# Three float16 products in the output projection of a gated attention block, and a later wait for its transposed attention

## The reference

```
x   : [8, 256, 128]      context : [8, 512, 128]      16 heads of 64
xn  = layernorm(layernorm(x)) ; q = xn @ w_q ; k, v = split(context @ w_kv)
attn = softmax((q * 64**-0.5) @ k.T)  per head
out  = (attn @ v).reshape(8, 256, 1024)                 # the attention
x   = x + tanh(g_xattn) * tanh(gate) * (out @ w_out + b_out)   # the output projection
tokens = layernorm(x) ; expert = argmax(tokens @ gate_w), at most 160 tokens for each of 8
x   = x + tanh(g_ffn) * prob * (relu(tokens @ w1[expert]) @ w2[expert])
```

## Time and profile before

| | |
|---|---|
| runs | 473.90, 474.88, 475.59 us, median 474.88 |
| profiled execution | 473.7 us from the first to the last instruction; what lies around the span is not recorded, so that the median is 1.2 us above it |
| TensorE matmul (PE) | busy 439.7 us, 93% of the span |
| ScalarE (ACT) | 386.4 us, 82% |
| VectorE (DVE) | 360.3 us, 76% |
| GpSimd (POOL) | 356.6 us, 75% |
| granted TensorE clock | 0.996 on average, full in all stretches of the attention |
| the chain that ended last | PE 40%, DVE 20%, ACT 16%, DMA 10%, issue 8%, POOL 4% |
| share of the 16 DMA engines' time with packets of the hardware queue | 93.4% |

### The profile page before, as it was taken

One profiled execution on the slowest core, in us unless ns is written; L12 is line 12 of the kernel. 1 busy time (PEld: TensorE's weight loads), 2 busy tenths in 40 slices (PEclk: granted clock), 3 DMA queues, 4 the chain that ended last, 5 costly groups with the idle time before them and its releaser, 6 DMA issues.

```text
span 473.7 us, 13155 instructions
## 1 busy us (share of the span) xinstructions
PE 439.7 (93%) x5096; PEld 334.0 (71%) x5096; DVE 360.3 (76%) x789; ACT 386.4 (82%) x630; POOL 356.6 (75%) x270
## 2 busy tenths in 40 slices
PE   7889799998999989999999999999999999988993
PEld 6656667776767767776777667776777677758892
DVE  4787687778877887779787796878877887785622
ACT  5889788899888988899888898899799998892330
POOL 3687686888788887888878877898878877871325
PEclk9999999999999999999999999999999999999998
DMA  5499999999999999999999999999989998996021
GB/s 167 150 177 192 206 187 175 170 181 204 188 176 188 210 194 180 192 192 192 198 189 197 189 196 191 185 200 209 190 157 185 193 180 147 159 182 137 14 67 46
DMA packets 283037, 82.10 MB, mean 173 GB/s; under 512 B 264387, under 2 KB 280435, under 8 KB 282976
## 3 DMA queue, kind: packets, MB, share of 16 engines
q1 hardware_dynamic: 281600, 77.96, 93.4%
q0 software_dynamic: 1376, 3.30, 2.2%
HBM read 10.83 MB, written 5.14 MB: 34 GB/s over the span
## 4 chain that ended last, share of the span: by engine, by line
PE 40%; DVE 20%; ACT 16%; DMA 10%; issue 8%; POOL 4%; POOLq 0%; SPq 0%; ACTq 0%; DVEq 0%
DVE MXL L903 9%; DMA PT<-PARTS 9%; ACT P L752 7%; DVE HL L890 4%; ACT HL L714 4%; PE psAB L1234 3%; PE psX L1319 3%; PE psAB L1241 3%; PE psO L1267 3%; ACT PARTS L762 3%; POOL PARTS L650 3%; PE psX L1355 3%; DVE VL L896 3%; PE psO L1269 3%; PE psO L1268 3%
## 5 line engine op out<-in xcount | busy, mean ns | idle before, releaser
L650 POOL TENSOR_TENSOR PARTS<-P,PARTS 128x1024 f16<-128x1024 f32 x125 | 267.4, 2145 | 63.5 <-ACT PARTS L762 61.8
L762 ACT ACTIVATE PARTS<-P 128x1024 f16<-128x1024 f32 x126 | 136.1, 1080 | 0.7
L752 ACT ACTIVATE P<-psAB,NB 128x512 f32<-128x512 f32 x128 | 81.6, 695 | 41.8 <-DVE NB L906 41.4
L903 DVE TENSOR_REDUCE MXL<-psAB 128x2 f32<-128x1024 f32 x64 | 78.4, 1224 | 41.4 <-PE psAB L1241 23.9
L1267 PE MATMUL psO<-VH,PT 128*128 128x65 f16 x1008 | 98.6, 194 | 8.3 <-DMA PT<-PARTS 7.7
L1267 PEld LDWEIGHTS psO<-VH,PT 128*128 128x128 f16 x1008 | 92.0, 98 | 12.0 <-DMA PT<-PARTS 8.9
L1268 PE MATMUL psO<-VL,PT 128*128 128x64 f16 x1008 | 98.5, 192 | 0.0
L1269 PE MATMUL psO<-VH,PT 128*128 128x65 f16 x1008 | 98.4, 193 | 0.0
L1268 PEld LDWEIGHTS psO<-VL,PT 128*128 128x128 f16 x1008 | 91.3, 98 | 0.5
L1269 PEld LDWEIGHTS psO<-VH,PT 128*128 128x128 f16 x1008 | 91.5, 97 | 0.0
L752 ACT ACTIVATE P<-psCD,NB 128x512 f32<-128x512 f32 x128 | 81.7, 703 | 0.1
(11 more groups left out here) (214 smaller groups left out, 871.7 us busy)
## 6 DMA issues: line engine op xcount, KB each, us to landing
ctx_raw<-in_ctx_dram SPq DMA_DIRECT2D x8, 256.0 KB, 3.7
w1s<-in_L_ffn_w_dram SPq DMA_DIRECT2D x8, 256.0 KB, 3.6
w2s<-in_L_ffn_w_dram SPq DMA_DIRECT2D x8, 256.0 KB, 4.0
PT<-PARTS SPq DMA_TRANSPOSE x126, 5.0
experts_table<-zeros POOLq DMA_DIRECT2D x2, 645.0 KB, 4.0
X<-in_x_dram SPq DMA_DIRECT2D x8, 128.0 KB, 4.2
wraw<-in_L_xattn_w_kv_dram SPq DMA_DIRECT2D x4, 256.0 KB, 5.3
out_dram<-row SPq DMA_DIRECT2D x8, 128.0 KB, 2.5
```

The lines of the kernel that those rows point to most:

```text
L650: pool.tensor_tensor(PARTS[:, par, qt, 1], P32[:, par, qt], PARTS[:, par, qt, 0], ALU.subtract).then_inc(plo_done, 1)
L752: last = act.activation(P32[:, par, qt, SK * h:SK * h + SK], score_bank(qt)[:, SK * h:SK * h + SK], ACT.Exp, bias=NB[:, par, qt, h:h + 1])
L762: act.activation(PARTS[:, hp % 2, qt, 0], P32[:, hp % 2, qt], ACT.Copy).then_inc(phi_done[qt], 1)
L903: dve.tensor_reduce(MXL[:, par, qt, :, 0], score_bank(qt)[:].rearrange("p (h n) -> p h n", h=2), AX.X, ALU.max, negate=True).then_inc(max_ ...
```

## The change

- Weights: `w_out` (float32, tile `wo`) is split once into two float16 tiles: `wo_hi` = 16 * wo rounded, made by ScalarE in slot 5 of batch 0, and `wo_lo` = 16 * wo - wo_hi, made by VectorE in slot 6 of batch 0 (128 x 1024 elements each).
- Attention: the ones column by which the sums of the softmax are taken becomes 1/16, so that the normalised attention comes 16 times as large. `ot_copy` writes its transpose in float16 (`OTH`), and a new VectorE instruction in each slot, `ot_low`, subtracts that from the PSUM bank and writes the rest in float16 (`OTL`). It stands after `normalise_heads` and ahead of `token_moments` and `x_moments`, and waits for `ot_done` of this same slot's copy.
- Products: each product of a 128 x 128 tile becomes three float16 matmuls (high x high, high x low, low x high). All wait for the low part (`ot_lo_done`), save the first two of the last two pairs.
- Scale: the projection is multiplied by `gproj` = gscale / 256, one small instruction more in slot 2 of batch 0.
- Order on TensorE: `k_project` no longer waits for the attention copy; `q_project` waits instead, and for the low part.

```diff
@@ pool
-            pool.memset(VH[:, :, :, DH:DH + 2], 1.0).then_inc(row_consts, 1)
+            pool.memset(VH[:, :, :, DH:DH + 2], 1.0 / O_LIFT).then_inc(row_consts, 1)
@@ scalar
-                act.activation(OT[:, QT * pair:QT * (pair + pairs), :], bank.rearrange("p (t c) -> p t c", c=P),
+                act.activation(OTH[:, QT * pair:QT * (pair + pairs), :], bank.rearrange("p (t c) -> p t c", c=P),
                                ACT.Copy).then_inc(ot_done, pairs)
...
+                    if hp == WO_HI_STEP and is_first(b):
+                        act.wait_ge(wo_in, 16)
+                        act.activation(wo_hi[:], wo[:], ACT.Copy, scale=WO_LIFT).then_inc(wo_hi_done, 1)
@@ vector
+            def ot_low(n, bank=psOT, pairs=1):
+
+                pair = n % PAIRS
+                dve.wait_ge(ot_done, n + pairs)
+                hi = OTH[:, QT * pair:QT * (pair + pairs), :]
+                dve.tensor_tensor(OTL[:, QT * pair:QT * (pair + pairs), :], bank.rearrange("p (t c) -> p t c", c=P), hi,
+                                  ALU.subtract).then_inc(ot_lo_done, pairs)
...
                     if VALUES_BEHIND <= j < LAST:
                         normalise_heads(*back(b, hp, VALUES_BEHIND))
+                    if ot_pair(j) >= 0:
+                        ot_low(ot_pair(j))
+                    if is_first(b) and hp == WO_LO_STEP:
+                        dve.wait_ge(wo_hi_done, 1)
+                        dve.scalar_tensor_tensor(out=wo_lo[:], in0=wo[:], scalar=WO_LIFT, in1=wo_hi[:], op0=ALU.mult,
+                                                 op1=ALU.subtract).then_inc(wo_lo_done, 1)
                     if hp == PROJECT_STEP and not is_first(b):
                         token_moments(b - 1)
...
             normalise_heads(B - 1, PAIRS - 1)
+            ot_low(LAST - 2)
             normalise_heads(B - 1, PAIRS - 2)
             add_part(B - 1, B, psEF)
+            ot_low(LAST - 1, psEF[:, 512:1024], 2)
@@ tensor, k_project and q_project
-                if ot_pair(j - AHEAD - 1) >= 0:
-                    pe.wait_ge(ot_done, ot_pair(j - AHEAD - 1) + 1)
                 pe.wait_ge(ctxt_lo_done, b + 1)
...
             def q_project(b, hp):
+                j = b * PAIRS + hp
                 q_cols = slice(P * hp, P * hp + P)
+                if ot_pair(j - AHEAD - 1) >= 0:
+
+                    pe.wait_ge(ot_lo_done, ot_pair(j - AHEAD - 1) + 1)
@@ tensor, project_part (project alike)
+            PRODUCTS = ((OTH, wo_hi), (OTH, wo_lo), (OTL, wo_hi))
+
+            def project_pairs(dst, qt, pairs):
+
+                for pair in pairs:
+                    for n, (o, w) in enumerate(PRODUCTS):
+                        last = pe.matmul(dst, o[:, pair * QT + qt, :], w[:, pair, :], start=(pair == pairs[0] and n == 0),
+                                         stop=(pair == pairs[-1] and n == len(PRODUCTS) - 1))
+                return last
...
-                pe.wait_ge(ot_done, b * PAIRS + pairs[-1] + 1)
-                pe.wait_ge(wo_in, 16)
+                pe.wait_ge(ot_lo_done, b * PAIRS + pairs[-1] + 1)
+                pe.wait_ge(wo_lo_done, 1)
                 for qt in range(QT):
-                    for pair in pairs:
-                        last = pe.matmul(bank[:, D * qt:D * qt + D], OT[:, pair * QT + qt, :], wo[:, pair, :],
-                                         start=(pair == pairs[0]), stop=(pair == pairs[-1]))
+                    last = project_pairs(bank[:, D * qt:D * qt + D], qt, pairs)
@@ tensor, project_last
+                for n, (o, w) in enumerate(PRODUCTS):
+                    if n == 0:
+                        pe.wait_ge(ot_done, b * PAIRS + PAIRS)
+                    elif o is OTL:
+                        pe.wait_ge(ot_lo_done, b * PAIRS + PAIRS)
+                    for qt in range(QT):
+                        for pair in pairs:
+                            last = pe.matmul([psX, psEF][qt][:, 0:D], o[:, pair * QT + qt, :], w[:, pair, :],
+                                             start=(pair == pairs[0] and n == 0),
+                                             stop=(pair == pairs[-1] and n == len(PRODUCTS) - 1))
```

More of the change, by code:

```diff
@@ L58, in gated_block @@
     LIFT = 7.0
+    O_LIFT, WO_LIFT = 16.0, 16.0
     AHEAD = 2
@@ L85, in gated_block @@
         gscale = sb("gscale", [P, 1], F32)
+        gproj = sb("gproj", [P, 1], F32)
         w_hi = sb("w_hi", [P, 3 * INNER], F32R)
@@ L88, in gated_block @@
         wo = sb("wo", [P, PAIRS, D], F32)
+        wo_hi = sb("wo_hi", [P, PAIRS, D], F16)
+        wo_lo = sb("wo_lo", [P, PAIRS, D], F16)
         bo = sb("bo", [P, D], F32)
@@ L116, in gated_block @@
         O = sb("O", [P, QT, INNER], F32)
-        OT = sb("OT", [P, QT * PAIRS, P], F32)
+        OTH = sb("OTH", [P, QT * PAIRS, P], F16)
+        OTL = sb("OTL", [P, QT * PAIRS, P], F16)
         stats = sb("stats", [P, TT, 6], F32)
@@ L261, in gated_block @@
         ot_done = sem("ot_done")
+        ot_lo_done = sem("ot_lo_done")
+        wo_hi_done = sem("wo_hi_done")
+        wo_lo_done = sem("wo_lo_done")
         proj_psum = sem("proj_psum")
@@ L403, in gated_block @@
         BO_STEP, BIAS_STEP = 2, 7
+        WO_HI_STEP, WO_LO_STEP = 5, 6
         ROUTE = 14
@@ L943, in add_part @@
                 dve.wait_ge(part_psum, part + 1)
+                dve.wait_ge(gscale_done, 2)
                 dve.wait_ge(part_done, part)
@@ L947, in add_part @@
                 dve.scalar_tensor_tensor(out=xs, in0=bank[:, 0:QT * D].rearrange("p (q d) -> p q d", q=QT),
-                                         scalar=gscale[:, 0:1], in1=xs, op0=ALU.mult, op1=ALU.add).then_inc(part_done, 1)
+                                         scalar=gproj[:, 0:1], in1=xs, op0=ALU.mult, op1=ALU.add).then_inc(part_done, 1)
             def token_moments(b):
@@ L1092, in batch @@
                         dve.wait_ge(gscale_done, 1)
+                        dve.tensor_scalar(gproj[:], gscale[:], 1.0 / (O_LIFT * WO_LIFT), None, ALU.mult).then_inc(gscale_done, 1)
                         dve.wait_ge(bo_in, 16)
@@ L1350, in project @@
                 wait_x((x1_done, b + 1))
-                pe.wait_ge(ot_done, b * PAIRS + PAIRS)
+                pe.wait_ge(ot_lo_done, b * PAIRS + PAIRS)
                 for qt in range(QT):
-                    dst = psX[:, D * qt:D * qt + D]
-                    for pair in range(PAIRS // 2, PAIRS):
-                        last = pe.matmul(dst, OT[:, pair * QT + qt, :], wo[:, pair, :], start=(pair == PAIRS // 2),
-                                         stop=(pair == PAIRS - 1))
+                    last = project_pairs(psX[:, D * qt:D * qt + D], qt, range(PAIRS // 2, PAIRS))
                 last.then_inc(proj_psum, 1)
@@ L1402, in batch @@
                             pe.wait_ge(kq_done, LAST + 1)
-                            pe.wait_ge(ot_done, ot_pair(j))
+                            pe.wait_ge(ot_lo_done, ot_pair(j))
                         o_transposes(ot_pair(j))
@@ L1437, in batch @@
                     values(b, PAIRS - 1)
-                    pe.wait_ge(ot_done, LAST - 2)
+                    pe.wait_ge(ot_lo_done, LAST - 2)
                     o_transposes(LAST - 2)
@@ L1441, in batch @@
                     project_part(b, range(PAIRS // 2, PAIRS - 2), psEF)
-                    pe.wait_ge(ot_done, LAST - 1)
+                    pe.wait_ge(ot_lo_done, LAST - 1)
                     o_transposes(LAST - 1, psEF[:, 512:1024], 2)
```

4 lines of the change are left out of this document (2 added, 2 removed).

## The result

The changed kernel takes 479.42 us (median of seven, 478.22 to 480.31) against 474.88 for the kernel before (473.32 to 477.87). The ratio is 1.0098, 95% interval 1.007 to 1.0127: it is slower by 3.3 to 6.0 us. The forecast was 479.4. The profiled execution of after took 478.22 us, its span is 476.4, and it is the fastest of the seven; before's profiled span is 473.7 us. So the two traces differ by only 2.7 us, and the medians by 4.5. The account of the prediction comes back to this.

The account below looks back on a forecast made before the run. Bound: the loop of scores, row maximum, low part, small task and values across TensorE and VectorE. Terms 5.7 - 0.8 + 1.1 + 0.8 - 1.8 - 0.5 = +4.5 us on 473.7, span 478.2, median 479.4; range 470.0 to 484.5.

Parts of the forecast that it names:

- The mechanism: VectorE, in order: the low part waits for ScalarE's same-slot copy and delays the next row maximum; 0.36 us after each copy.
- its sign: In the profile after, VectorE's wait for ScalarE's OTH copy should be some 10 to 20 us in all.
- Rival B: The low part's wait hides, all 15 projection halves gain 0.5 us: 468.2 us; chance 0.23 with its half-way case.
- The step for slot 0: Slot 0: copy ends 5.95 us after the row maximum's start, plus 0.36 gives 6.31 against 5.98, a loss of 0.33.
- 0.2 a batch: VectorE, running later, waits less for the high part of the values; 0.2 us taken off the batch's sum.
- Rival D: Projection's float16 matmuls slower than taken, deciding from 0.079 us each; 483.6 us with no gain in a half; chance 0.10.
- 5.7 - 0.8 - 1.8: Batches 1 to 6: +5.7 us at 0.95 each, -0.8 without x moments in batch 6, -1.8 hidden in transpose waits.
- absorption in waits for transposes: Where TensorE's wait for DMA transposes sets a group of slots, the new wait hides: 0.5 in three or four batches, -1.8 us.
- the end +0.1: Last batch and end: shorter products, a low part of 512 columns, slots without value work; -0.5 us, 1.5 of doubt either way.
- the prediction's own last step: From span to median: the runs' median is 1.2 us above the profiled span, so 478.2 becomes 479.4 us.
- The weight split: Batch 0: VectorE's 1024-column instruction costs 0.8 us, part of the copy's wait using up idle time; ScalarE's costs nothing.
- Rival C: Landing of transposes sets the pace once TensorE is faster and hides the new wait: no change, 474.9 us; chance 0.14.

Follow-up runs that it names:

- run without the products: Changed kernel with the float32 products of the kernel before and no weight split, low part still made and waited for; 482.86 us, ratio 1.0172 to the kernel before.
- products alone: Changed kernel without any low-part instruction on VectorE, the third product taking the high part of the attention again; 472.4 us, ratio 0.9988 to the kernel before.
- run with the constant tile: The products-only version plus a VectorE instruction of the low part's size reading constant SBUF tiles, without the copy's wait; 501.09 us, ratio 1.0576 to the kernel before.

## Why the prediction was right, point by point

**The mechanism** was the forecast one: VectorE's in-order wait for this slot's copy. The low part starts 0.03 us behind the copy, shown above for slots 4 and 7, and the M that ends slots 2 to 5, 7 and 0 comes straight behind it or behind the moments. VectorE's wait for the copy is 27.9 us in all, more than the 10 to 20 that the prediction named as its sign. Rival B, the wait hides, falls by the run without the products: 1.0172 in place of 1 or a little over.

**The slots.** Forecast and measured (the batch above, or where it is not typical the other batches): slot 1 7.05 and 6.90; slot 2 6.71 and 6.71; slot 3 7.05 and 7.08; slot 4 6.62 and 6.62; slot 5 5.80 and 5.73; slot 6 6.03 and 6.02 (6.23 here); slot 7 6.95 and 6.89; slot 0 6.31 and 6.05. The step for slot 0 failed: it took the copy to end 5.95 after M as in the earlier trace rows, but 0.28 of that came from a short slot 7. ScalarE had the high part of the values late, VectorE waited for it, and in slot 0 the attention copy in turn waits for VectorE, which has to read the keys and queries out of the same bank (L900, done at 229.38, the copy at 229.46). With slot 7 long the copy ends 5.67 after M (229.84 less 224.17; low part at 229.88). The same step had been made for slot 5 and not for slot 0. Slot 1 is 0.15 shorter than forecast, as the projection starts 2.06 after M (180.07 less 178.01), not 2.18, and is 0.05 shorter itself. The start is earlier because VectorE, running later, finds the high part of the values there: its wait for that fell from 8.2 us in 16 waits to 3.1 in 3, by 5.1, where the forecast took off 0.2 a batch. With the products alone, where M of slot 1 isn't late, the start was still 2.18 after it and the slot 7.03.

**The products.** Timeline of TensorE in slot 1 of that batch, first and last of 24 matmuls, and the first of the values product:

```profile
180.07 0.23 PE L1351 MATMUL psX<-wo_hi,OTH 128*128 128x128 f16 x1 [0.28 <-DVE VL L910]
...
181.36 0.22 PE L1351 MATMUL psX<-wo_hi,OTL 128*128 128x128 f16 x1
181.42 0.19 PE L1301 MATMUL psO<-VH,PT 128*128 128x65 f16 x1
```

A half takes 1.35 us, forecast 1.40, by 0.056 per matmul (1.29 / 23), forecast 0.058. Scaling a float16 pace by columns held. Rival D would have needed 0.079. The figure of the Trainium skill that stood in the prediction (TensorE: Matmul & The Clock Gate, section Back-to-back issue gap: about 81 ns for 128 columns) doesn't hold here; the trace decides for 0.056.

**The terms of the sum** are less good than the total. From M of slot 1 to M of the next slot 1, after less before, the batches 0 to 6 gave +2.1, -0.8, -0.8, +0.9, +0.6, +0.9 and -0.1 us; the last batch and the tail together +0.1. For batches 1 to 6 that is +0.7, where the forecast had 5.7 - 0.8 - 1.8 = +3.1. The term that was mis-sized is the absorption in waits for transposes. Slot 7 of batches 1 and 2 was already 7.48 and 7.38 us long in before, by such a wait, and so got shorter (6.89) where +1.28 was forecast for a typical one. The traced batch, with slot 7 at 5.67, was the wrong one to multiply by six. Batch 0 gave +2.1, forecast +1.9, and the end +0.1, forecast -0.5. With the first slots 0.2 shorter, the sum over the trace is thus +2.7 and not +4.5.

That the median came out as forecast is luck, and the prediction's own last step shows where it lies. It put the median 1.2 us above the span of one execution, because before's profiled span of 473.7 was set beside the median of other executions. Wherever a run on record has both numbers of one execution, its time is 1.8 to 2.2 us above its span. By that, before's profiled execution took about 475.6 us, 0.7 above the median, and after's is 1.2 below its own. The seven spans of after have a median of 477.4. So the forecast span of 478.2 was 0.8 us too long and the step of 1.2 was 0.8 too short, and the two errors cancel. The direction and the mechanism are shown; the sum isn't.

**The weight split** in batch 0 cost about twice the 0.8 us of the forecast. Within batch 0, which has no projection, the run without the products is the changed kernel less the split. Its slot 6 takes 5.79 us, after's 7.47, and slots 5, 7 and 0 agree to 0.02. VectorE at the end of that slot, after first and then the run without the products:

```profile
59.77 0.42 DVE L943 TENSOR_TENSOR OTL<-psEF,OTH 128x256 f16<-128x256 f32 x1 [0.90 <-ACT OTH L752]
60.11 1.50 DVE L1110 SCALAR_TENSOR_TENSOR wo_lo<-wo,wo_hi 128x1024 f16<-128x1024 f32 x1
61.53 1.21 DVE L917 TENSOR_REDUCE MXL<-psAB 128x2 f32<-128x1024 f32 x1
```

```profile
60.11 0.42 DVE L938 TENSOR_TENSOR OTL<-psEF,OTH 128x256 f16<-128x256 f32 x1 [0.44 <-ACT OTH L750]
60.65 1.23 DVE L912 TENSOR_REDUCE MXL<-psAB 128x2 f32<-128x1024 f32 x1
```

The prediction had two steps wrong here. It let the copy's wait eat most of VectorE's part, but the split stands behind that wait and delays M by all of its 1.42 us, less 0.20 that M waits without it. And it put ScalarE's part at nothing, though `wo_hi` takes 1.07 us: the exponentials of slot 6 start 1.88 us after M, and the low part starts 5.71 us after M, 0.46 later than without the split. Together that is 1.68, the measured difference. That the batch as a whole came near the forecast is again luck: slots 7 and 0, forecast 1.1 us longer, are 0.3 longer (12.48 against 12.15).

**Rival C** was half right, on a kernel that isn't the changed one: with the products alone, slots held by late transposes did take back the gain.

## What to carry to other kernels

Ask of a new instruction on an in-order engine not how long it is but what it waits for and who is queued behind it: 25 us of VectorE work didn't show in the time, and the wait for a copy of the same slot cost over 1%. Put independent work (here the moments) between the wait and its releaser, and look at every batch, not one typical one, for slots that are already held by something else. Before moving a wait to another engine, list what it has to wait for there and what stands behind it: here that cost 2.3% more. And set a profiled span beside the time of the same execution only, not beside a median of others.

## What the runs showed of the hardware

An elementwise VectorE instruction of 256 float32 columns took 0.42 us with one operand in PSUM and, in the rows below, up to 1.89 with both in SBUF. VectorE and then GpSimd in the run with the constant tile:

```profile
198.94 1.89 DVE L945 TENSOR_TENSOR OTL<-zeros 128x256 f16<-128x256 f32 x1
...
206.36 1.26 DVE L945 TENSOR_TENSOR OTL<-zeros 128x256 f16<-128x256 f32 x1
...
213.32 0.41 DVE L945 TENSOR_TENSOR OTL<-zeros 128x256 f16<-128x256 f32 x1
```

```profile
198.41 2.14 POOL L661 TENSOR_TENSOR PARTS<-P,PARTS 128x1024 f16<-128x1024 f32 x1 [1.69 <-ACT PARTS L773]
200.77 2.14 POOL L661 TENSOR_TENSOR PARTS<-P,PARTS 128x1024 f16<-128x1024 f32 x1 [0.22 <-ACT PARTS L773]
...
205.18 2.15 POOL L661 TENSOR_TENSOR PARTS<-P,PARTS 128x1024 f16<-128x1024 f32 x1 [0.70 <-ACT PARTS L773]
```

The two long ones end at 200.83 and 207.62, 0.28 and 0.29 us after GpSimd's instruction (200.55 and 207.33), which had started first. The short one, 0.41 us, ran while GpSimd stood still. GpSimd's own mean hardly moved (2181 ns, 2149 in after). The Trainium skill, SBUF — State Buffer, section SBUF: two separate sides, has it that a VectorE instruction with two SBUF inputs and a GpSimd instruction that reads SBUF exclude each other for their whole length, and that the first to start holds the ports. These rows agree for a GpSimd instruction that starts first; they show none where VectorE does.
